# Two additions of exponentials per group, moved from GpSimd to VectorE in 30 groups

## The chip, the cores and the metric

The kernel runs on one core of a Trainium2 chip. The metric is the device time of one execution in microseconds (us). Engines: TensorE (PE, with its weight loads as PEld), VectorE (DVE), ScalarE (ACT), GpSimd (POOL), and SyncE (SP), which starts the DMAs.

## The reference

One transformer layer on 2048 tokens of width 512: the normalised tokens go through causal attention (16 heads of 32) and beside it through a feed-forward part with 4-bit weights; both are added to the input. The change lies in the attention:

```
scores = einsum('bhqd,bhkd->bhqk', q, k) * scale
scores = where(causal, scores, finfo.min)
probs = softmax(scores, axis=-1)          # exp(s - row max) / sum over keys
attn = einsum('bhqk,bhkd->bhqd', probs, v)
x = x + attn @ w_o.T + ffn(xn)
```

The sum over the keys in the softmax is what is divided by: one number for each query and head. The additions of this document make it.

## The kernel before, in words

Three stages follow one another: normalisation and the projections (up to about 140 us of the span), attention (to about 727 us), and the output projection with the feed-forward part.

**Attention** works on 8 pairs of heads. Within a pair, `STEPS` lists 40 steps: for each of four chunks of 512 queries (`qc`), the tiles of 128 keys (`kt`) up to the diagonal. Four steps make a **group** (`GS`), so there are 80 groups, 0 to 79, ten for each pair. Groups 0, 2, 5 and 9 of a pair are **diagonal**: they hold the four key tiles that the causal mask cuts, and their steps get narrower (512, 384, 256, 128 queries).

In each step, for each head of the pair: TensorE makes the transposed scores, keys by queries (`scores_t`, line 1041, on the diagonal with a mask, line 1050), in three PSUM banks; ScalarE takes exponentials into one of 16 buffers `e_sb` (`exps`, line 819), one group ahead of what follows; TensorE multiplies them with V (`product_v`, line 1067). Step j of group k+1 is scored and exponentiated while TensorE is in group k.

**The row maxima** that the exponentials need come from a second set of scores, queries by keys, made up to 48 products ahead: the units. TensorE writes a unit into one of four banks of `p_s` (`scores`, line 1013), VectorE takes its maximum over the keys (`unit_max`, line 902, or 898 with the mask), and only then is the bank free (`bank_free`). Eight units fall to a group, spread by `some_units` over the group's transposed scores, seven before the products by V and the last behind them. Group 72 has six and 73 to 79 have none. When the maxima of a chunk are complete, VectorE joins them (`row_max`, line 909), GpSimd splits them into three bf16 parts in five small operations (`split`, lines 751 to 759), and TensorE turns them (line 1023).

**The row sums.** Exponentials are first added elementwise over the steps of a group, and only the sum goes through TensorE (`row_sums`, line 1084, against ones). The list `ADDS[k]` has the additions of group k, each for one head (0 or 1) in turn. A group off the diagonal has four: numbers 0 and 1 add steps 0 and 1, numbers 2 and 3 add steps 2 and 3, and VectorE then **joins** the two halves for each head (`join_sums`, line 957). A diagonal group has six: 0 and 1 add the part of step 0 that step 1 covers and step 1, and 2 to 5 add steps 2 and 3 into the same sum, in place; there is no join. The sums lie in six slots (`SUM_BUFS`), and an addition that starts a sum waits till its slot has been read (`needs`). GpSimd does the additions (line 736) in groups with units. In groups without units VectorE does half of them (line 947).

**Order of the work.** Each engine's program is written out in a loop over the groups and runs in that order. GpSimd in turn k: additions from number 2 on of group k, additions 0 and 1 of group k+1, splits, and in some groups of pairs 2, 4, 6 and 7 a normalisation of an earlier pair's result (line 770). VectorE in turn k: the maxima of the group's units, the join before the last one, joined row maxima, its own additions. ScalarE overwrites a buffer only when the addition that read it is done (`used_up`). In the last groups VectorE also divides (`divide`, lines 929 and 934) and splits the output weights (line 985), and GpSimd splits the attention result (line 775).

## Time and profile before

| | us |
|---|---|
| median of three runs | 1799.53 (1797.9 to 1799.81) |
| the profiled execution | 1800.45, span 1798.7 |
| TensorE busy | 1763.6 (98%) |
| VectorE busy | 1237.7 (69%) |
| GpSimd busy | 752.2 (42%) |
| ScalarE busy | 715.2 (40%) |
| GpSimd's additions of exponentials, line 736 (the form from two buffers) | 304.4, 244 of them |

The table is over all three stages. In the 40 slices of the page, attention is about slices 5 to 16; there GpSimd's tenths are 8, VectorE's 8 and 9, TensorE's 9. Shares over the whole span hide that. In a timeline row the first number is the start, the second the length, both in us; `x2` is two instructions in one row, whose length is from the start of the first to the end of the last, and the bracket at the end is idle time of the engine before it and what ended it. In rows of waits the numbers are the total, the count and the longest.

### The profile page before, as it was taken

Reading aid. Unit: us, or ns where it says so; the run is one execution under the profiler, and the core shown is the slowest. Engines: PE = TensorE matmul, PEld = TensorE weight load, DVE = VectorE, ACT = ScalarE, POOL = GpSimd, SP = SyncE. Lnnn points to the kernel's source line nnn. Section 1 sums busy time; section 2 is a strip of 40 time slices with the busy share of each in tenths; the row PEclk is TensorE's granted clock in tenths of the full one; section 3 lists DMA queues with packets and bytes.
Section 4 is the critical chain, followed back from the end, with each engine's and each line's share of the span. In section 5 each row is a group of like instructions: output and inputs, shape, how many; then the busy total and the mean of one; then the engine's idle time right before and its main releaser. Section 6 shows DMA issues by size and latency. Waiting matters only on the chain.

```text
span 1798.7 us, 28378 instructions
## 1 busy us (share of the span) xinstructions
PE 1763.6 (98%) x10176; PEld 1346.1 (75%) x10176; DVE 1237.7 (69%) x1834; ACT 715.2 (40%) x1171; POOL 752.2 (42%) x716
## 2 busy tenths in 40 slices
PE   7999999999999999999999999999999999999998
PEld 6886666656556556888888888888888888888887
DVE  5526888888888889686676567567567666666654
ACT  3324666666666665233223232323233223222322
POOL 1432888888888886122122222222222222222221
PEclk9999999999999999999999999999999999999999
DMA  8775044144143111511110110110110010010002
GB/s 280 223 230 156 10 105 84 28 105 84 29 105 83 29 40 60 182 30 36 35 35 0 35 35 0 35 35 0 35 35 14 21 35 28 7 35 0 1 1 94
DMA packets 75615, 108.55 MB, mean 60 GB/s; under 512 B 24912, under 2 KB 44992, under 8 KB 72384
## 3 DMA queue, kind: packets, MB, share of 16 engines
q1 hardware_dynamic: 75520, 107.34, 22.1%
q8 instruction: 53, 0.87, 0.2%
q14 instruction: 42, 0.34, 0.1%
HBM read 74.04 MB, written 29.59 MB: 58 GB/s over the span
## 4 chain that ended last, share of the span: by engine, by line
PE 59%; DVE 0%; ACT 0%; issue 0%; ACTq 0%
PE p_up L52 7%; PE p_v L52 7%; PE p_up L51 7%; PE p_v L51 7%; PE p_up L50 7%; PE p_v L50 7%; PE p_s L51 6%; PE p_s L52 6%; PE p_s L50 6%; PE p_s L345 0%; PE p_s L339 0%; PE p_s L340 0%; PE p_v L339 0%; PE p_v L345 0%; PE p_v L340 0%; PE p_up L339 0%
## 5 line engine op out<-in xcount | busy, mean ns | idle before, releaser
L1392 POOL TENSOR_SCALAR poly<-poly 128x1024 f32<-128x1024 f32 (+1 forms) x65 | 72.4, 1114 | 800.8 <-ACT poly L1349 800.8
L736 POOL TENSOR_TENSOR e_sum<-e_sb 128x512 f32<-128x512 f32 (+1 forms) x244 | 304.4, 1271 | 75.5 <-ACT e_sb L819 39.1
L902 DVE TENSOR_REDUCE max_part<-p_s 128x1 f32<-128x512 f32 x384 | 247.1, 683 | 62.2 <-PE p_s L1013 61.3
L819 ACT ACTIVATE e_sb<-p_v 128x512 f32<-128x512 f32 (+3 forms) x427 | 216.1, 549 | 119.6 <-PE p_v L1041 59.1
L1455 DVE SCALAR_TENSOR_TENSOR inter<-inter,gate 128x1024 f32<-128x1024 f32 (+1 forms) x65 | 78.6, 1209 | 241.1 <-ACT inter L1355 240.3
L50 PE MATMUL p_v<-xn_hi,w_hi 128*128 128x512 f32 x512 | 199.2, 389 | 0.0
L51 PE MATMUL p_v<-xn_lo,w_hi 128*128 128x512 f32 x512 | 199.2, 389 | 0.0
L52 PE MATMUL p_v<-xn_hi,w_lo 128*128 128x512 f32 x512 | 199.2, 389 | 0.0
L50 PE MATMUL p_up<-xn_hi,w_hi 128*128 128x512 f32 x512 | 199.2, 389 | 0.0
L51 PE MATMUL p_up<-xn_lo,w_hi 128*128 128x512 f32 x512 | 199.2, 389 | 0.0
L52 PE MATMUL p_up<-xn_hi,w_lo 128*128 128x512 f32 x512 | 199.2, 389 | 0.0
L1348 ACT ACTIVATE gate<-p_v 128x1024 f32<-128x1024 f32 (+1 forms) x65 | 66.0, 1015 | 332.7 <-PE p_v L52 332.7
L50 PE MATMUL p_s<-stack_hi,w_hi 128*128 128x512 f32 x504 | 196.1, 389 | 0.0
L51 PE MATMUL p_s<-stack_lo,w_hi 128*128 128x512 f32 x504 | 196.1, 389 | 0.0
L52 PE MATMUL p_s<-stack_hi,w_lo 128*128 128x512 f32 x504 | 196.1, 389 | 0.0
L1395 POOL TENSOR_TENSOR poly<-poly,gate 128x1024 f32<-128x1024 f32 (+1 forms) x65 | 179.5, 2761 | 5.4
L1067 PE MATMUL p_o<-e_sb,v_stack 128*32 128x256 f32 (+1 forms) x2304 | 149.4, 374 | 0.0
L1355 ACT ACTIVATE inter<-poly 128x1024 f32<-128x1024 f32 (+1 forms) x65 | 68.1, 1047 | 202.3 <-POOL poly L1395 202.3
L1475 DVE TENSOR_TENSOR acc<-acc,p_s 128x2048 f32<-128x2048 f32 x63 | 143.7, 2280 | 3.3 <-PE p_s L52 3.3
L898 DVE CUSTOM_DVE_ANT_0 recip<-p_s,score_mask 128x128 bf16<-128x128 f32 (+3 forms) x256 | 115.8, 485 | 37.2 <-PE p_s L1013 36.4
L819 ACT ACTIVATE e_sb<-p_st 128x512 f32<-128x512 f32 (+2 forms) x213 | 117.3, 551 | 58.2 <-PE p_st L1041 30.3
L1360 ACT ACTIVATE stack_hi<-inter 128x1024 fp32r<-128x1024 f32 (+1 forms) x65 | 68.1, 1048 | 163.0 <-DVE inter L1461 163.0
(190 smaller groups left out, 3486.7 us busy)
## 6 DMA issues: line engine op xcount, KB each, us to landing
k_stack<-qk_scratch SPq DMA_DIRECT2D x42, 256.0 KB, 7.6
qk_scratch<-out_hi SPq DMA_DIRECT2D x32, 256.0 KB, 2.6
qk_scratch<-out_lo SPq DMA_DIRECT2D x32, 256.0 KB, 3.3
q_stack<-qk_scratch SPq DMA_DIRECT2D x24, 256.0 KB, 6.5
xn_lo_scratch<-xn_lo SPq DMA_DIRECT2D x4, 1024.0 KB, 5.2
v_stack<-in_gate_up_s SPq DMA_DIRECT2D x64, 64.0 KB, 2.3
xn_lo<-xn_lo_scratch SPq DMA_DIRECT2D x4, 1024.0 KB, 13.8
scales<-in_gate_up_s SPq DMA_DIRECT2D x64, 64.0 KB, 2.5
```

The costliest lines, as they stand in the source:

```text
L50: nc.tensor.matmul(out, w_hi, x_hi, start=first, stop=False)
L51: nc.tensor.matmul(out, w_hi, x_lo, start=False, stop=False)
L52: return nc.tensor.matmul(out, w_lo, x_hi, start=False, stop=last)
L736: nc.gpsimd.tensor_tensor(*operands(k, i), ALU.add).then_inc(pool_summed, 1)
L819: nc.scalar.activation(e_sb[:, x % E_BUFS, 0:w], bank_st(x)[:, 0:w], ACT.Exp, scale=SCALE).then_inc(exp_done, 1)
L898: nc.vector.tensor_tensor_reduce(out=masked_scores[:, m % 2, 0:w], in0=p_s[:, slot[n] % S_BUFS, 0:w], in1=score_mask[:, W - w:], scale=1.0 ...
L902: nc.vector.reduce_max(part, p_s[:, slot[n] % S_BUFS, 0:w], AX.X).then_inc(maxed, 1)
L1067: last = nc.tensor.matmul(p_o[(2 * a + h) * D:(2 * a + h + 1) * D, 0, first - h * HALF:], v_stack[p % PB][:, kt, a, :], e_sb[:, (g * PIECE ...
L1392: nc.gpsimd.tensor_scalar(part_of(poly, h, parts), part_of(poly, h, parts), GELU_A, 1.0, ALU.mult, ALU.add).then_inc(poly_done, 1)
L1395: nc.gpsimd.tensor_tensor(part_of(poly, h, parts), part_of(poly, h, parts), part_of(gate, h, parts), ALU.mult).then_inc(poly_done, 1)
L1455: nc.vector.scalar_tensor_tensor(part_of(inter, h, parts), part_of(inter, h, parts), 1.0, part_of(gate, h, parts), ALU.add, ALU.mult).then ...
L1475: nc.vector.tensor_tensor(here, here, p_out[:, :, :], ALU.add).then_inc(added, 1)
```

## The change

VectorE makes additions 0 and 1 of group k+1 in front of the last maximum of group k, where group k is diagonal and has units (`EARLY[k + 1]`). In such a group GpSimd makes all the others. Where a group is not `EARLY`, the share is as before: that is, VectorE's own additions in groups 74 to 79. In group 73, which is `EARLY` and has no units, VectorE makes 0 and 1 instead of 2 and 3. Additions in place wait for the engine that made the one before (`needs` now gives the semaphore with the count).

```
--- before.py
+++ after.py
@@ -429,6 +429,8 @@
 
 
 
+
+    EARLY = [k > 0 and DIAG[GS * (k - 1) % NS] and len(units_of(k - 1)) > 0 for k in range(NG)]
     ADDS, first_sum, sum_group, made, added_to = [], [], [], {}, []
     by_pool = by_vector = 0
     for k in range(NG):
@@ -440,7 +442,7 @@
         first_sum.append(len(sum_group))
         sum_group += [k] * (2 if diag else 4)
         for i, (m, a, _, _) in enumerate(ADDS[k]):
-            vector = not units_of(k) and (a == 1 if diag else m >= 2)
+            vector = i < 2 if EARLY[k] else not units_of(k) and (a == 1 if diag else m >= 2)
             by_vector += vector
             by_pool += not vector
             made[k, i] = (vector, by_vector if vector else by_pool)
@@ -568,13 +570,14 @@
             m, a, _, x = ADDS[k][i]
             n = first_sum[k] + m
             if x is None:
-                return None, made[k, i - 2][1]
+                vector, count = made[k, i - 2]
+                return None, (vector_summed if vector else pool_summed, count)
             if n < SUM_BUFS:
-                return None, 0
+                return None, None
             group = sum_group[n - SUM_BUFS]
             if not DIAG[GS * group % NS] and n - SUM_BUFS < first_sum[group] + 2:
-                return (joined, JOINED_TO[group]), 0
-            return (rows_done, group + 1), 0
+                return (joined, JOINED_TO[group]), None
+            return (rows_done, group + 1), None
 
         def operands(k, i):
             m, a, y, x = ADDS[k][i]
@@ -588,7 +591,7 @@
             return e_sum[:, n % SUM_BUFS, 0:W - q0], e_sb[:, ((GS * k + x) * PIECES + a) % E_BUFS, skip:skip + W - q0], new
 
         def pooled_to(k, i):
-            return max(count for j in range(i + 1) for vector, count in [made[k, j]] if not vector)
+            return max([added_to[k - 1][0]] + [count for j in range(i + 1) for vector, count in [made[k, j]] if not vector])
 
 
         def v_slot(v):
@@ -732,7 +735,7 @@
                         if free:
                             pool.wait_ge(*free)
                         if earlier:
-                            pool.wait_ge(pool_summed, earlier)
+                            pool.wait_ge(*earlier)
                         nc.gpsimd.tensor_tensor(*operands(k, i), ALU.add).then_inc(pool_summed, 1)
 
             def split(p, r, before):
@@ -934,8 +937,8 @@
                         nc.vector.tensor_tensor(attn_rows(p, a, qc)[:, h * HALF:(h + 1) * HALF], o[rows, 0, :],
                                                 recip[rows, 0:HALF], ALU.mult).then_inc(divided, 1)
 
-            def sum_steps(k):
-                for i in range(len(ADDS[k])):
+            def sum_steps(k, part):
+                for i in range(len(ADDS[k]))[part]:
                     vector, count = made[k, i]
                     if vector:
                         dve.wait_ge(exp_done, exps_for(k, i))
@@ -943,7 +946,7 @@
                         if free:
                             dve.wait_ge(*free)
                         if earlier:
-                            dve.wait_ge(vector_summed, earlier)
+                            dve.wait_ge(*earlier)
                         nc.vector.tensor_tensor(*operands(k, i), ALU.add).then_inc(vector_summed, 1)
 
             def join_sums(k):
@@ -970,11 +973,13 @@
                 for n in units:
                     if n == units[-1]:
                         join_sums(k)
+                        if k + 1 < NG and EARLY[k + 1]:
+                            sum_steps(k + 1, slice(0, 2))
                     unit_max(n)
                     for p_, r in BATCHES[k]:
                         if n + 1 == p_ * NU + UNITS_TO[r]:
                             join_parts(p_, r)
-                sum_steps(k)
+                sum_steps(k, slice(2 if EARLY[k] else 0, None))
                 if not units:
                     join_sums(k)
                 if p == PAIRS - 1 and s in (20, 24, 28):
```

VectorE's instructions where group 10 (diagonal) ends and group 11 begins, before. Line 902 and 898 are maxima, 957 is the join, `max_part` 128x1 the second half of 898:

```order
L902 TENSOR_REDUCE max_part<-p_s 128x1 [waits scored] x6
L898 ISA recip,max_part<-p_s,score_mask 128x384 [waits maxed,scored]
L898 ISA max_part 128x1
L898 ISA recip,max_part<-p_s,score_mask 128x384 [waits maxed,scored]
L898 ISA max_part 128x1
L902 TENSOR_REDUCE max_part<-p_s 128x1 [waits scored]
L957 TENSOR_TENSOR e_sum<-e_sum 128x512 [waits pool_summed]
L957 TENSOR_TENSOR e_sum<-e_sum 128x512
L902 TENSOR_REDUCE max_part<-p_s 128x1 [waits scored]
```

The same place in the changed kernel, where the lines are 905, 901 and 960, and 950 is an addition of exponentials:

```order
L905 TENSOR_REDUCE max_part<-p_s 128x1 [waits scored]
L950 TENSOR_TENSOR e_sum<-e_sb 128x512 [waits rows_done,exp_done] x2
L905 TENSOR_REDUCE max_part<-p_s 128x1 [waits scored] x5
L901 ISA recip,max_part<-p_s,score_mask 128x384 [waits maxed,scored]
L901 ISA max_part 128x1
L901 ISA recip,max_part<-p_s,score_mask 128x384 [waits maxed,scored]
L901 ISA max_part 128x1
L905 TENSOR_REDUCE max_part<-p_s 128x1 [waits scored]
L960 TENSOR_TENSOR e_sum<-e_sum 128x512 [waits vector_summed,pool_summed]
L960 TENSOR_TENSOR e_sum<-e_sum 128x512
L905 TENSOR_REDUCE max_part<-p_s 128x1 [waits scored]
```

Two additions of group 11 stand in front of the last maximum of group 10; the rest keeps its order.

GpSimd at the same place, before: the two rows of additions in place of group 10, all four additions of group 11, and additions 0 and 1 of group 12 (128x384):

```order
L736 TENSOR_TENSOR e_sum<-e_sum,e_sb 128x256 [waits pool_summed,exp_done] x2
L736 TENSOR_TENSOR e_sum<-e_sum,e_sb 128x128 [waits pool_summed,exp_done] x2
L736 TENSOR_TENSOR e_sum<-e_sb 128x512 [waits rows_done,exp_done] x4
L736 TENSOR_TENSOR e_sum<-e_sb 128x384 [waits rows_done,exp_done] x2
```

And now (line 739), where additions in place of group 10 wait for VectorE's sums:

```order
L739 TENSOR_TENSOR e_sum<-e_sum,e_sb 128x256 [waits vector_summed,exp_done] x2
L739 TENSOR_TENSOR e_sum<-e_sum,e_sb 128x128 [waits pool_summed,exp_done] x2
L739 TENSOR_TENSOR e_sum<-e_sb 128x512 [waits rows_done,exp_done] x2
L739 TENSOR_TENSOR e_sum<-e_sb 128x384 [waits rows_done,exp_done] x2
```

Additions 2 and 3 of group 11 are left in one row of two.

VectorE at the end of the maxima, in groups 72 to 74, before. Line 985 splits output weights:

```order
L898 ISA max_part 128x1
L898 ISA recip,max_part<-p_s,score_mask 128x512 [waits maxed,scored]
L898 ISA max_part 128x1
L909 TENSOR_REDUCE row_max<-max_part 128x2x4 [waits max_split,maxed]
L985 TENSOR_TENSOR stack_lo<-wo_sb,stack_hi 128x512 [waits wo_hi_made]
L947 TENSOR_TENSOR e_sum<-e_sb 128x512 [waits rows_done,exp_done] x2
L957 TENSOR_TENSOR e_sum<-e_sum 128x512 [waits vector_summed,pool_summed]
L957 TENSOR_TENSOR e_sum<-e_sum 128x512
L985 TENSOR_TENSOR stack_lo<-wo_sb,stack_hi 128x512 [waits wo_hi_made]
```

And now, with lines 990 for the weights and 912 for `row_max`:

```order
L901 ISA recip,max_part<-p_s,score_mask 128x512 [waits maxed,scored]
L901 ISA max_part 128x1
L950 TENSOR_TENSOR e_sum<-e_sb 128x512 [waits joined,exp_done] x2
L901 ISA recip,max_part<-p_s,score_mask 128x512 [waits maxed,scored]
L901 ISA max_part 128x1
L912 TENSOR_REDUCE row_max<-max_part 128x2x4 [waits max_split,maxed]
L990 TENSOR_TENSOR stack_lo<-wo_sb,stack_hi 128x512 [waits wo_hi_made]
L960 TENSOR_TENSOR e_sum<-e_sum 128x512 [waits vector_summed,pool_summed]
L960 TENSOR_TENSOR e_sum<-e_sum 128x512
L990 TENSOR_TENSOR stack_lo<-wo_sb,stack_hi 128x512 [waits wo_hi_made]
```

The additions of group 73 stand in front of the last masked maximum, and the join of group 73 follows directly on a weight split.

## Rows read from the trace of the kernel before

**Rows 1.** busy us (instructions) of each engine in one window; columns as headed

```profile
core 0: us, PE busy (x) PEld busy (x) DVE busy (x) ACT busy (x) POOL busy (x), PEclk, DMA share, GB/s
230.00:300.00 70.00, 68.58 (x638) 42.19 (x637) 59.88 (x137) 44.61 (x96) 55.84 (x71) 1.00 0.36 77
```

**Rows 2.** TensorE's waits, 178 to 716 us: total, times, longest us

```profile
PE p_s L1013 <- DVE max_part L898: 3.3, 7, 0.7
PE p_s L1013 <- DVE max_part L902: 1.5, 3, 0.5
```

**Rows 3.** timeline of VectorE at the ends of groups 9, 10, 12, 15

```profile
start us, us, engine line op out<-in xcount [idle before <-releaser]
241.15 0.69 DVE L902 TENSOR_REDUCE max_part<-p_s 128x1 f32<-128x512 f32 x1 [2.49 <-PE p_s L1013]
...
247.53 0.69 DVE L902 TENSOR_REDUCE max_part<-p_s 128x1 f32<-128x512 f32 x1 [1.67 <-PE p_s L1013]
...
260.74 0.29 DVE L898 CUSTOM_DVE_ANT_0 recip<-p_s,score_mask 128x128 bf16<-128x128 f32 x1 [1.26 <-PE p_s L1013]
...
261.61 0.42 DVE L898 CUSTOM_DVE_ANT_0 recip<-p_s,score_mask 128x256 bf16<-128x256 f32 x1 [0.57 <-PE p_s L1013]
...
280.54 0.69 DVE L902 TENSOR_REDUCE max_part<-p_s 128x1 f32<-128x512 f32 x1 [1.39 <-PE p_s L1013]
```

**Rows 4.** timeline of ScalarE (group 11's exponentials), then GpSimd

```profile
244.26 1.15 ACT L819 ACTIVATE e_sb<-p_v 128x512 f32<-128x512 f32 x2
245.22 0.68 ACT L819 ACTIVATE e_sb<-p_st 128x512 f32<-128x512 f32 x1
...
243.03 5.00 POOL L736 TENSOR_TENSOR e_sum<-e_sb 128x512 f32<-128x512 f32 x4 [0.87 <-ACT e_sb L819]
...
280.48 5.01 POOL L736 TENSOR_TENSOR e_sum<-e_sb 128x512 f32<-128x512 f32 x4
```

**Rows 5.** timeline of TensorE in groups 11, 12, then VectorE in 12

```profile
249.12 0.48 PE L1013 MATMUL p_s<-k_stack,q_stack 96*128 96x512 f32 x1
...
249.84 0.38 PE L1041 MATMUL p_st<-q_stack,k_stack 128*128 128x256 f32 x1
...
256.59 0.63 PE L1013 MATMUL p_s<-k_stack,q_stack 96*128 96x512 f32 x2
...
255.32 2.48 DVE L902 TENSOR_REDUCE max_part<-p_s 128x1 f32<-128x512 f32 x4
```

**Rows 6.** timeline, GpSimd and VectorE at group 17; then all joins, grouped

```profile
290.92 2.98 POOL L736 TENSOR_TENSOR e_sum<-e_sb 128x512 f32<-128x512 f32 x2 [1.60 <-PE p_o L1084]
...
291.24 3.20 DVE L957 TENSOR_TENSOR e_sum<-e_sum 128x512 f32<-128x512 f32 x2
...
L957 DVE TENSOR_TENSOR e_sum<-e_sum 128x512 f32<-128x512 f32 x96 | 106.3, 1146 | 1.0 <-POOL e_sum L736 0.2
```

**Rows 7.** timeline of GpSimd and VectorE in group 26

```profile
349.32 5.46 POOL L736 TENSOR_TENSOR e_sum<-e_sb 128x512 f32<-128x512 f32 x4
...
351.89 3.45 DVE L957 TENSOR_TENSOR e_sum<-e_sum 128x512 f32<-128x512 f32 x2
```

**Rows 8.** timeline of TensorE: groups 27 and 28, and 18

```profile
355.99 0.51 PE L1013 MATMUL p_s<-k_stack,q_stack 96*128 96x512 f32 x1 [0.50 <-DVE max_part L902]
...
363.13 0.50 PE L1013 MATMUL p_s<-k_stack,q_stack 96*128 96x512 f32 x1 [0.67 <-DVE max_part L898]
...
294.98 0.50 PE L1013 MATMUL p_s<-k_stack,stack_lo 96*128 96x512 f32 x1 [0.30 <-DVE max_part L898]
```

**Rows 9.** timeline of VectorE, GpSimd, TensorE at attention's end

```profile
667.57 1.30 DVE L947 TENSOR_TENSOR e_sum<-e_sb 128x512 f32<-128x512 f32 x2
...
670.80 3.43 DVE L947 TENSOR_TENSOR e_sum<-e_sb 128x512 f32<-128x512 f32 x2
...
678.45 0.56 DVE L947 TENSOR_TENSOR e_sum<-e_sb 128x384 f32<-128x384 f32 x1 [1.33 <-PE p_o L1084]
...
667.12 0.61 POOL L751 CAST max_cols<-row_max 128x8 bf16<-128x8 f32 x1 [2.89 <-DVE row_max L909]
...
670.28 3.40 POOL L736 TENSOR_TENSOR e_sum<-e_sb 128x512 f32<-128x512 f32 x2
...
711.37 1.08 PE L1084 MATMUL p_o<-e_sum,ones 128*32 128x256 f32 x8 [3.00 <-DVE e_sum L957]
```

More of the change, by code:

```diff
@@ L425, in attention @@
     slot = {what: n for n, what in enumerate(ring)}
+    EARLY = [k > 0 and DIAG[GS * (k - 1) % NS] and len(units_of(k - 1)) > 0 for k in range(NG)]
     ADDS, first_sum, sum_group, made, added_to = [], [], [], {}, []
@@ L442, in attention @@
         for i, (m, a, _, _) in enumerate(ADDS[k]):
-            vector = not units_of(k) and (a == 1 if diag else m >= 2)
+            vector = i < 2 if EARLY[k] else not units_of(k) and (a == 1 if diag else m >= 2)
             by_vector += vector
@@ L570, in needs @@
             if x is None:
-                return None, made[k, i - 2][1]
+                vector, count = made[k, i - 2]
+                return None, (vector_summed if vector else pool_summed, count)
             if n < SUM_BUFS:
-                return None, 0
+                return None, None
             group = sum_group[n - SUM_BUFS]
             if not DIAG[GS * group % NS] and n - SUM_BUFS < first_sum[group] + 2:
-                return (joined, JOINED_TO[group]), 0
-            return (rows_done, group + 1), 0
+                return (joined, JOINED_TO[group]), None
+            return (rows_done, group + 1), None
         def operands(k, i):
@@ L590, in pooled_to @@
         def pooled_to(k, i):
-            return max(count for j in range(i + 1) for vector, count in [made[k, j]] if not vector)
+            return max([added_to[k - 1][0]] + [count for j in range(i + 1) for vector, count in [made[k, j]] if not vector])
         def v_slot(v):
@@ L734, in sum_steps @@
                         if earlier:
-                            pool.wait_ge(pool_summed, earlier)
+                            pool.wait_ge(*earlier)
                         nc.gpsimd.tensor_tensor(*operands(k, i), ALU.add).then_inc(pool_summed, 1)
@@ L935, in divide, with sum_steps @@
                                                 recip[rows, 0:HALF], ALU.mult).then_inc(divided, 1)
-            def sum_steps(k):
-                for i in range(len(ADDS[k])):
+            def sum_steps(k, part):
+                for i in range(len(ADDS[k]))[part]:
                     vector, count = made[k, i]
@@ L945, in sum_steps @@
                         if earlier:
-                            dve.wait_ge(vector_summed, earlier)
+                            dve.wait_ge(*earlier)
                         nc.vector.tensor_tensor(*operands(k, i), ALU.add).then_inc(vector_summed, 1)
@@ L972, in _ @@
                         join_sums(k)
+                        if k + 1 < NG and EARLY[k + 1]:
+                            sum_steps(k + 1, slice(0, 2))
                     unit_max(n)
@@ L976, in _ @@
                             join_parts(p_, r)
-                sum_steps(k)
+                sum_steps(k, slice(2 if EARLY[k] else 0, None))
                 if not units:
```

## The prediction

> **What bounds the kernel now.** I read the views from coarse to fine. A 70 us window in the middle of the attention stage [rows 1] shows TensorE busy for 68.58 us at full granted clock, VectorE for 59.88, GpSimd for 55.84: TensorE bounds the stage, VectorE has some 10 us in 70 left, GpSimd 14. Next, TensorE's waits between 178 and 716 us: its scores wait 4.8 us in all for VectorE's maxima (3.3 and 1.5, [rows 2]), and once, at 711.37, it waits 3.00 us for a join of VectorE's [rows 9]. TensorE is almost never held up by GpSimd, so relief of GpSimd brings nothing by itself. It can only help through VectorE, and VectorE is the engine that gets the work. So the question is where VectorE has room, and how much lateness TensorE forgives.
>
> **What is removed, added and moved.** Groups are numbered 0 to 79, ten for each pair of heads. In the 30 groups whose forerunner is diagonal and has maxima (1, 3, 6, then 10, 11, 13, 16, 20, 21, ...) additions 0 and 1 pass to VectorE. In group 73 VectorE in turn gives up additions 2 and 3. By the lists of additions that the program makes, GpSimd goes from 368 to 310 and VectorE from 16 to 74. VectorE does the two right before the last maximum of the diagonal group. There it idles today until TensorE, busy with the products by V, sends the last score: 2.49 us in group 9, 1.67 in group 10, 1.26 in group 12, 1.39 in group 15, and the same in every later pair [rows 3].
>
> **Price of two additions.** Where GpSimd is not adding, two of 128x512 take VectorE 1.30 us (at 667.57, [rows 9]). Where VectorE is not, four take GpSimd 5.00 us, so two 2.5 (at 243.03, [rows 4]). When both add at once they take turns: GpSimd started at 290.92 and took 2.98 for two, VectorE started 0.32 us later and took 3.20 for two [rows 6]. So the pair on VectorE costs 1.30 us or 3.20 us, depending on whether GpSimd is adding at that moment. A mean over all joins would be neither.
>
> The Trainium skill (SBUF — State Buffer, "Who interferes with whom") says that a VectorE instruction with two inputs in SBUF and a GpSimd instruction that reads SBUF block one another whole, and that whoever is first decides. By a reading in which both merely slow down, the pair would cost 2 x 1.146 = 2.3 us (the mean join in the window's list, [rows 6]), VectorE would be 0.6 us late after group 10, and nothing would be lost there. By the skill's rule it is the 3.2 us above. The rows at 290.92 and 291.24 agree with the rule, with 3.20 us.
>
> **Groups 9, 12 and 15: no cost.** In 9 there is 2.49 us of room. In 12 the additions start as VectorE gets free, 1.26 us before the score, and overrun by 0.04 us, and the next idle time is 0.57 us [rows 3]. In 15 they fit, 1.30 into 1.39. GpSimd does not collide here: after its own diagonal additions it has the splitting of the maxima, which waits for VectorE's row_max and lasts till 280.48 (small operations), and only then additions [rows 4]. If that cover is gone, each costs like group 10.
>
> **Group 10: the loss.** GpSimd has no splitting here. Freed of additions 0 and 1 of group 11 (today it does all four in one run, from 243.03 to 248.03), it starts addition 2 when its exponentials are there: ScalarE finishes them at 245.4 and 245.9 [rows 4]. VectorE gets free at 245.86 (247.53 less 1.67 of idle time, [rows 3]), 0.4 us after GpSimd has begun: the situation of 290.92 again. So 3.20 us from 245.8, to 249.0; the last maximum starts at 249.0 and not at 247.53, about 1.4 us late.
> TensorE writes scores into four banks, so the fourth score of group 11 (249.12) needs the bank of that maximum (ended 248.22): room 0.90 us. I allow 0.05 from the end of a maximum to the score behind it and take 0.05 off the lateness for rounding: 1.35 + 0.05 - 0.90, about 0.5 us of wait. ScalarE's wait at 249.84 (0.12 us, [rows 5]) is swallowed by it, so 0.36 is left. VectorE's remaining lateness against TensorE is then about 0.6 us (1.4 less what TensorE waited, less the short idle times between maxima), and I let 0.15 of it go in the rest of group 11: 0.45. In group 12 the sixth score (256.83, the second of the pair of matmuls at 256.59) stands 0.21 behind the end of its maximum (256.62, the second of four from 255.32, [rows 5]): 0.45 + 0.05 - 0.21 = 0.29 us more. Sum 0.65 us in each of eight places (groups 0, 10, ..., 70): **+5.2 us**. Bounds: 0, if the two run unhindered (1.30 < 1.67); and 1.4 us each, 11.2 us, if none of the lateness is forgiven.
>
> **Odd pairs: the gain.** In group 26 (also 46 and 66) GpSimd is behind today because it also normalises: additions of 26 and 27 from 349.32 to 354.8, across VectorE's join of 26, which takes 3.45 us where two operations alone would take 1.3 [rows 7]. TensorE pays 0.50 us at 355.99, and at 363.13 it pays 0.67 where the even pair pays 0.30 (294.98) [rows 8]. Without additions 0 and 1 of group 26 (2.5 us) the rest starts some 2 us earlier, and the additions of 27 end near 352.5. The join still meets the end of one, and then the normalisation, but ends some 0.5 us earlier. Value 0.50 + 0.37 = 0.87 us, three times: **-2.6 us**. Bounds: 0 (the normalisation, itself an addition-like operation, merely takes the place of the additions) and all of the 4.8 us that scores wait for maxima [rows 2].
>
> **The end of attention.** There are no maxima from group 73 on, and VectorE does half of the additions, both joins and the divisions. From 678.45 on it shows no idle time until its last join, for which TensorE waits 3.00 us [rows 9]. Whatever reaches 678.45 late comes out at the end, less 1.33 us of idle time there. Additions 0 and 1 of group 73 move in front of the last maximum of group 72, where VectorE idles like in the other diagonal groups, and cost nothing. But additions 2 and 3 now lie with GpSimd, behind the splitting (from 667.12; about 1.8 us once VectorE's two additions no longer lie across it) and take 2.5: until 671.4. The join of 73 starts then, not right behind VectorE's own additions at 668.9, and in turns with GpSimd's additions of 74, so 3.4 us (the price that additions 2 and 3 of group 74 pay today, [rows 9]) to 674.8. Behind it on VectorE are a split of the output weights (with the normalisation ahead of it on GpSimd, to 676.7), two additions (1.3), the join of 74 (1.3) and another weight split (0.6): 679.8. So the work of 678.45 starts 1.35 us late, and the 3.00 us become about 4.4: **+1.4 us**. TensorE itself needs the join of 73 only in front of the products of group 74, whose row sums release VectorE at 678.45, so that has room. Bounds: -3.0 (the wait disappears) and +3.4 (the whole shift).
>
> Nothing else moves the end: the row sums of the diagonal groups find their additions earlier than today, and DMAs are not touched.
>
> **Sum.** +5.2 - 2.6 + 1.4 = +4.0 us. The profiled execution took 1800.45 us (span 1798.7); with +4.0 it would take 1804.5. The median of the runs is 0.9 lower, 1799.53: **1803.5 us**, 0.22% slower. About 0.2% (3.6 us) is what a measurement of this kernel can tell from no change.
>
> **The rivals.**
> 1. The additions on VectorE are free, since they fall into its idle time: group 10 costs nothing. For it: the 58 additions at 0.65 are 38 us, and rows 3 show idle time at each place. Against it: 0.4 us head start of GpSimd. Time: 1799.5 - 2.6 + 1.4 = 1798.3, no change to be measured.
> 2. Relief of GpSimd wins: the joins no longer meet its additions in odd pairs, and the end of attention is reached without the last wait, because VectorE has two additions fewer there. -2.6 - 3.0 = -5.6: 1793.9, faster. It decides if GpSimd finishes additions 2 and 3 of group 73 before about 669.5. Against it: they stand behind the splitting, which ends near 669 at the earliest.
> 3. The lateness is not forgiven: each place costs 1.4 us, and the end takes the full 3.4: 1799.5 + 11.2 + 3.4 - 2.6 = 1811.5. It would take VectorE to be late in groups 11 and 12 with no idle time to recover; against it, the idle times of 1.26 and 0.57 us in group 12.
> 4. The change does not do what it says, as the exponentials of the next group come too late and VectorE waits in front of its last maximum: the exponentials it needs are finished 1 us before [rows 4]; I give it nothing of its own.
>
> **Chances.** Forecast 0.52 (its own range 1801 to 1806.5), rival 1 0.27, rival 2 0.09, rival 3 0.12. The range 1797.5 to 1809 takes in rival 1 and half of rival 3. Slower by over 0.2% (above 1803.1): half of the forecast's case and more, and rival 3: 0.47. Faster (below 1795.9): 0.10. Within: 0.43.
>
> **What the changed profile would show.** Right: VectorE's two additions in group 10 take near 3.2 us, with GpSimd's first addition of group 11 started before them, while those in groups 12 and 15 take 1.3; TensorE's waits on maxima have new entries of about 0.5 us near 249 and every 67 us on, and 0.3 near 257; the 0.50 at 355.99 is gone or halved; the 3.00 on the last join is above 4. Wrong: the additions in group 10 take 1.3 us (then rival 1), the last wait is shorter than 3.0 (rival 2), or waits of over 0.5 us stand in groups 13 to 16 too (rival 3).

## The result and the profile after

The changed kernel takes 1804.7 us (median of seven runs, 1803.9 to 1806.05), against 1799.53 before: ratio 1.0031, 95% interval 1.0019 to 1.0042. It is 5.2 us slower. Its profiled execution spans 1802.9 us, 4.2 more than the one before.

The same 70 us window as in [rows 1] of the changed kernel (columns: busy us and instructions of PE, PEld, DVE, ACT, POOL, then granted clock, DMA share, GB/s):

```profile
230.00:300.00 70.00, 68.04 (x629) 42.27 (x632) 65.85 (x146) 44.62 (x96) 47.68 (x62) 1.00 0.35 76
```

VectorE went from 59.88 to 65.85 us of 70, GpSimd from 55.84 to 47.68. TensorE, which bounds the stage, lost 0.54 us of work in the window. (VectorE's busy time includes what an addition waits for its turn inside its row, so the 6 us more are not all work.)

TensorE's waits for maxima, 178 to 700 us, in the changed kernel (total, times, longest), where [rows 2] had 3.3 and 1.5 us:

```profile
PE p_s L1018 <- DVE max_part L905: 3.0, 10, 0.3
PE p_s L1028 <- DVE max_part L905: 2.7, 14, 0.2
PE p_s L1018 <- DVE max_part L901: 2.3, 7, 0.3
```

The second row is the matmul that turns the row maxima (line 1028, before 1023). [rows 2] leave it out; before, in the same stretch, it was

```profile
PE p_s L1023 <- DVE max_part L902: 1.3, 7, 0.2
```

All waits for maxima together went from 6.1 to 8.0 us.

The place of the forecast loss, VectorE in groups 10 and 11 (timeline: start, length, us):

```profile
246.02 3.23 DVE L950 TENSOR_TENSOR e_sum<-e_sb 128x512 f32<-128x512 f32 x2
249.17 3.07 DVE L905 TENSOR_REDUCE max_part<-p_s 128x1 f32<-128x512 f32 x5
```

GpSimd there:

```profile
245.73 2.96 POOL L739 TENSOR_TENSOR e_sum<-e_sb 128x512 f32<-128x512 f32 x2 [3.78 <-ACT e_sb L822]
```

and TensorE:

```profile
247.23 0.50 PE L1018 MATMUL p_s<-k_stack,q_stack 96*128 96x512 f32 x1
...
249.90 0.50 PE L1018 MATMUL p_s<-k_stack,q_stack 96*128 96x512 f32 x1 [0.34 <-DVE max_part L905]
...
252.39 0.38 PE L1028 MATMUL p_s<-ident_bf,max_cols 128*64 128x128 bf16 x4 [0.20 <-DVE max_part L905]
...
254.56 0.50 PE L1018 MATMUL p_s<-k_stack,q_stack 96*128 96x512 f32 x1
```

GpSimd begins 0.29 us before VectorE, the two then take turns, and VectorE's pair takes 3.23 us. It runs straight into the last maximum of group 10, where there had been 1.67 us of idle time. TensorE waits 0.34 us for the bank, and 0.20 more at the matmul that turns the row maxima. To see what a group costs I compare when TensorE sends its last score. Those of groups 10 and 11 were sent at 246.99 and 253.85 before and at 247.23 and 254.56 now: 0.24 and 0.71 us later, a step of about 0.46 us in group 11. It returns within 0.01 us in groups 21, 31, 41, 51, 61 and 71. I call such a difference from one group to the next a **step**. The steps of the attention stage with maxima are: +0.46 seven times, +0.76 three times (groups 25, 45, 65), -0.62 to -0.66 three times (27 and 28, 47 and 48, 67 and 68, together), +0.08 once. Sum +3.6 us. Steps also leave out what differs before attention: the last score of group 0 lies between 1.07 us earlier and 2.35 us later than before in the profiled executions of this document.

The step of +0.76 was not forecast. VectorE and GpSimd in groups 22 to 24 of the changed kernel:

```profile
327.55 1.30 DVE L950 TENSOR_TENSOR e_sum<-e_sb 128x512 f32<-128x512 f32 x2
...
340.61 2.90 DVE L960 TENSOR_TENSOR e_sum<-e_sum 128x512 f32<-128x512 f32 x2 [0.82 <-POOL e_sum L739]
```

```profile
327.47 0.22 POOL L754 CAST max_cols<-row_max 128x8 bf16<-128x8 f32 x1 [5.36 <-DVE row_max L912]
327.77 0.53 POOL L756 TENSOR_TENSOR rest<-row_max,max_cols 128x8 f32<-128x8 f32 x1
328.37 0.56 POOL L758 CAST max_cols<-rest 128x8 bf16<-128x8 f32 x1
...
338.06 4.90 POOL L739 TENSOR_TENSOR e_sum<-e_sb 128x512 f32<-128x512 f32 x4
```

GpSimd now idles 5.36 us in front of the splitting of the maxima, which waits for VectorE's `row_max`. The additions taken from it would have filled that time; its work behind does not start earlier. On the contrary: VectorE's pair at 327.55 lies across the splitting, whose second and third operation take 0.53 and 0.56 us in place of 0.20 and 0.22. GpSimd reaches the additions of group 24 later, and VectorE's join of 24 waits 0.82 us and then meets GpSimd's next additions: 2.90 us, where it took 2.10 without a wait before. TensorE, 1.23 us behind the kernel before at that time, is 1.98 us behind at the same matmul of group 25 (344.08 before, 346.06 now).

The end of attention. VectorE's join of group 73, GpSimd before it, and TensorE's last waits:

```profile
675.27 3.43 DVE L960 TENSOR_TENSOR e_sum<-e_sum 128x512 f32<-128x512 f32 x2 [3.71 <-POOL e_sum L739]
```

```profile
671.03 0.61 POOL L754 CAST max_cols<-row_max 128x8 bf16<-128x8 f32 x1 [7.68 <-DVE row_max L912]
...
672.71 5.44 POOL L739 TENSOR_TENSOR e_sum<-e_sb 128x512 f32<-128x512 f32 x4
```

```profile
716.04 0.64 PE L1089 MATMUL p_o<-e_sum,ones 128*32 128x256 f32 x8 [3.75 <-DVE e_sum L960]
...
718.61 0.30 PE L1089 MATMUL p_o<-e_sb,ones 128*32 128x128 f32 x2 [0.42 <-DVE e_sum L950]
```

The join waits 3.71 us for GpSimd, whose additions 2 and 3 of group 73 stand behind the splitting, and takes 3.43. Against [rows 9] TensorE's wait went from 3.00 to 3.75, with 0.42 behind it (`only3` below, whose end of attention is as before, has 0.49 there too). These two executions can't be compared directly, though, as the granted clock shows (columns as above, before and then after, 668 to 676 us, and 708 to 716 or 712 to 720):

```profile
668.00:676.00 8.00, 6.92 (x44) 3.02 (x44) 7.79 (x9) 5.00 (x11) 6.92 (x7) 0.79 0.20 77
708.00:716.00 8.00, 5.00 (x55) 2.64 (x48) 7.69 (x10) 0.00 (x0) 5.01 (x4) 0.79 0.46 134
```

```profile
668.00:676.00 8.00, 7.31 (x74) 3.68 (x65) 3.71 (x9) 5.51 (x11) 4.68 (x8) 1.00 0.59 183
678.00:686.00 8.00, 7.56 (x61) 4.62 (x61) 7.90 (x7) 5.07 (x12) 6.50 (x6) 0.79 0.01 2
712.00:720.00 8.00, 3.84 (x55) 2.12 (x48) 7.69 (x10) 0.00 (x0) 4.96 (x4) 1.00 0.51 147
```

The execution before had two stretches at 1.2 GHz at the end of attention, the one after had one, so part of the loss is hidden in the pair of profiles: 4.2 us there, 5.2 between the medians.

### The profile page after: what moved, and what is told of

Read it like the earlier page. It is cut to its first block, busy times and chain, and to the rows that moved or that the text cites. A ratio compares the mean times of both kernels' runs of the same rounds, so it can differ in the third digit from the quotient of the medians.

```text
span 1802.9 us, 28450 instructions
## 1 busy us (share of the span) xinstructions
PE 1764.1 (98%) x10176; PEld 1345.8 (75%) x10176; DVE 1284.4 (71%) x1892; ACT 716.1 (40%) x1171; POOL 693.6 (38%) x658
## 4 chain that ended last, share of the span: by engine, by line
PE 59%; DVE 0%; ACT 0%; issue 0%; ACTq 0%
PE p_v L50 6%; PE p_up L50 6%; PE p_up L52 6%; PE p_v L51 6%; PE p_v L52 6%; PE p_up L51 6%; PE p_s L50 6%; PE p_s L52 6%; PE p_s L51 6%; PE p_s L340 0%; PE p_s L339 0%; PE p_s L345 0%; PE p_v L339 0%; PE p_v L340 0%; PE p_v L345 0%; PE p_up L339 0%
## 5 line engine op out<-in xcount | busy, mean ns | idle before, releaser
L739 POOL TENSOR_TENSOR e_sum<-e_sb 128x512 f32<-128x512 f32 (+1 forms) x186 | 237.3, 1301 | 81.7 <-ACT e_sb L822 50.5
L1447 DVE SCALAR_TENSOR_TENSOR w_lo<-weight,w_hi 128x1024 fp32r<-128x1024 f32 x48 | 92.4, 1926 | 56.9 <-ACT w_hi L1346 56.9
```

Source lines behind the costliest of these rows:

```text
L739: nc.gpsimd.tensor_tensor(*operands(k, i), ALU.add).then_inc(pool_summed, 1)
L1447: nc.vector.scalar_tensor_tensor(w_lo[par][:, m, :, :], weight[:, :, :], CODE_SCALE, w_hi[par][:, m, :, :].bitcast(F32), ALU.mult, ALU.sub ...
```

## The experiments

Each is an edit of the changed kernel, compared with the kernel before run on the same chip. Times are compared by their medians, which is good to about 2 us from one kernel to another; steps are good to 0.05 us where the clock is the same. The medians mix executions with more and with fewer stretches at 1.2 GHz. Of the kernel before, measured beside the first four experiments, 19 executions with a mean granted clock of 0.999 have a median of 1797.91 us, and four with 0.997 have 1801.17. That is as much as most effects here, so the argument rests on steps and rows first. The first ones choose the groups with the early pair by a condition in one line:

```
-    EARLY = [k > 0 and DIAG[GS * (k - 1) % NS] and len(units_of(k - 1)) > 0 for k in range(NG)]
+    EARLY = [k > 0 and DIAG[GS * (k - 1) % NS] and len(units_of(k - 1)) > 0 and CONDITION for k in range(NG)]
```

**The second groups alone** (`only1`, CONDITION `k % 10 == 1`).

> VectorE makes additions 0 and 1 early only in the second group of each pair (1, 11, 21, ..., 71). Theory (the two engines' additions exclude one another, and GpSimd's head start of 0.4 us makes VectorE's pair cost 3.3 us in place of 1.3): TensorE falls behind by 0.46 us in each of groups 11, 21, ..., 71 and nowhere else, so +3.2 us against the kernel before, about 1802.8. Rival (the cost is spread over all 58 moved additions, 5.2 us / 58 each): 16 of them make +1.4 us, 1801.0, with steps of TensorE elsewhere too. Rival (free in idle time): 1799.5.

Measured: 1801.87 against 1799.0, ratio 1.0020 (1.0010 to 1.0029). The steps are 0.46 us in groups 11, 21, ..., 71, and nowhere else is there one above 0.06. The +2.9 us (interval 1.8 to 5.2) fit 7 x 0.46 = 3.2; a cost spread over all additions gave 1.4 and steps elsewhere too.

**All but the second groups** (`no1`, CONDITION `k % 10 != 1`).

> The change without the second groups of the pairs. Theory: the seven steps of 0.46 us go, 1804.7 - 3.2 = 1801.5; the step of 0.76 us in groups 25, 45 and 65 stays. Rival (spread over all additions): 1804.7 - 1.4 = 1803.3.

Measured: 1802.45, ratio 1.0019 (1.0008 to 1.0031). The seven steps are gone and +0.73, +0.70, +0.73 in groups 25, 45, 65 remain. The time fell by 2.2 us, between the two expectations; the steps decide for the theory.

**The same work without overlap** (`held1`).

```
                         if earlier:
                             pool.wait_ge(*earlier)
+                        if EARLY[k] and k % 10 == 1 and i == 2:
+                            pool.wait_ge(vector_summed, made[k, 1][1])
```

> The changed kernel, and in groups 1, 11, ..., 71 GpSimd's addition 2 waits until VectorE has made its two. The same work with no overlap. Theory: VectorE's pair takes 1.3 us, fits in 1.67 us, TensorE's step of 0.46 us in 11, 21, ... vanishes: 1804.7 - 3.2 = 1801.5, unless GpSimd, 1.8 us later, now meets the join of group 11. Rival (VectorE is late for another reason than GpSimd's additions: exponentials, slots, or its own load): the step stays, 1804.7.

Measured: 1801.97, ratio 1.0019 (1.0010 to 1.0029); 2.7 us less than the changed kernel. VectorE and GpSimd in group 10:

```profile
246.03 1.28 DVE L952 TENSOR_TENSOR e_sum<-e_sb 128x512 f32<-128x512 f32 x2
247.79 0.69 DVE L907 TENSOR_REDUCE max_part<-p_s 128x1 f32<-128x512 f32 x1 [0.48 <-PE p_s L1020]
```

```profile
247.48 4.61 POOL L741 TENSOR_TENSOR e_sum<-e_sb 128x512 f32<-128x512 f32 x4 [5.52 <-PE p_o L1091]
```

The pair takes 1.28 us in place of 3.23, 0.48 us of idle time are left in front of the maximum, and there is no step in 11, 21, ..., 71. VectorE does as many additions as in the changed kernel, and GpSimd starts its own 1.75 us later. So it is the overlap, not VectorE's load, that cost 0.46 us. Nor were the exponentials late (rival 4): the pair starts without idle time, at 246.02 and at 246.03.

**The seventh groups alone** (`only6`, CONDITION `k % 10 == 6`).

> VectorE makes additions 0 and 1 early only in the seventh group of each pair (6, 16, 26, ..., 66). Theory: no step against TensorE; the joins of 26, 46 and 66 get less in the way of GpSimd, and TensorE gains 0.6 us (as in the changed kernel) to 0.87 us (as forecast) three times: 1799.5 - 1.9 to 2.6, about 1797.3. Rival (relief of GpSimd brings nothing, what was gained in groups 27 and 28 of the changed kernel is only the 0.76 us lost before, partly given back): 1799.5.

Measured: 1796.02 against 1799.0, ratio 0.9984 (0.9975 to 0.9994): faster. Steps -0.52 and -0.35 us in groups 27 and 28, -0.50 and -0.36, -0.54 and -0.34 in the later ones: -0.87 each time, which is the forecast term. VectorE's join of group 26, then TensorE's first wait behind it:

```profile
350.79 2.94 DVE L960 TENSOR_TENSOR e_sum<-e_sum 128x512 f32<-128x512 f32 x2
```

```profile
361.16 0.50 PE L1018 MATMUL p_s<-k_stack,q_stack 96*128 96x512 f32 x1 [0.33 <-DVE max_part L901]
```

The join takes 2.94 us where it took 3.45 [rows 7]; of TensorE's waits in [rows 8] the 0.50 is gone and the 0.67 is 0.33. The rival falls.

**The fourth groups alone** (`only3`, CONDITION `k % 10 == 3 and k < 73`).

> VectorE makes additions 0 and 1 early only in the fourth groups (3, 13, 23, ..., 63). Theory (in these groups GpSimd idles before the splitting anyway, so it gains nothing; VectorE's pair lies across the splitting and lengthens it by 0.7 us; in pairs 2, 4 and 6, where GpSimd also normalises, this reaches the join of 24, 44, 64): TensorE falls behind by 0.75 us in groups 25, 45, 65, and the 0.50 and 0.67 us of groups 27 and 28 do not get smaller: 1799.0 + 2.2 = 1801.2. Rival (the step comes from all of GpSimd's altered order together, the late groups 21 and 22 above all): no step in 25, 1799.0.

Measured: 1799.13 against 1799.41, ratio 0.9999 (0.9990 to 1.0009). The steps of +0.77, +0.71, +0.75 in groups 25, 45, 65 are there, so the fourth groups make them. But groups 27, 47 and 67 give back 0.60, 0.53 and 0.58, which I had not expected. TensorE, held up in 25, no longer waits in 27; I read it as one wait in place of the other, which no run isolates. (A step of +1.67 in group 28 is a stretch at 1.2 GHz at 365 us.)

**All but the fourth groups** (`no3`, CONDITION `k % 10 != 3 or k == 73`).

> The change without the fourth groups (3, 13, ..., 63). Theory (the step of 0.75 us in 25, 45, 65 comes from them and eats the gain of groups 26, 46, 66): that step goes, and the waits in 27 and 28 fall by 0.87 us as in the kernel that changes the seventh groups alone: TensorE's balance in each of these pairs changes from +0.14 to -0.87, 1804.7 - 3.0 = 1801.7. Rival (the parts add up: the fourth groups alone changed nothing that can be measured): 1804.7.

Measured: 1802.29 against 1799.88, ratio 1.0019 (1.0008 to 1.0029). No step in 25, and -0.86, -0.85, -0.85 in groups 27 and 28, 47 and 48, 67 and 68. Two small ones appear in 58 and 69 (+0.3 each). 2.4 us less than the changed kernel, where 3.0 were expected: the gain of the seventh groups had been eaten by the fourth, though the fourth alone change nothing that can be measured. What makes the two small steps is open.

**Group 73 alone** (`only73`, CONDITION `k == 73`).

> Only group 73 is changed: VectorE makes 0 and 1 in front of the last maximum of group 72, GpSimd makes 2 and 3. Theory (the join of 73 waits 3.7 us for GpSimd, and the lateness reaches the last join less the idle time at 678): TensorE's 3.0 us wait for the join of group 78 becomes 3.8 to 4.4, 1799.0 + 0.8 to 1.4 = about 1800.1. Rival (VectorE has two additions fewer behind the maxima): the wait falls below 3.0, under 1799.0.

Measured: 1803.51 against 1799.41, ratio 1.0019 (1.0008 to 1.0030), between 1.4 and 5.4 us by the interval; more than expected. Part of that is the clock: six of the ten executions have a granted clock of 0.996 or 0.997 (1802.97 to 1807.09 us), and the four with 0.998 or more have a median of 1800.81, 1.5 us above the 20 such executions of the kernel before (1799.28). TensorE's wait for the last join is 6.15 us in the profile, but that is the slowest of the ten, with stretches at 1.2 GHz at 503, 673 and 714 us.

**All but group 73** (`no73`, CONDITION `k != 73`).

> The change without group 73. Theory (the late join of 73 costs 2.1 to 2.7 us at the end of attention where TensorE's clock is not halved): 1804.7 - 2.4 = 1802.3; TensorE's only large wait there is 3.0 to 3.3 us for the last join. Rival (the end costs 1.4 us, as forecast): 1803.3. Rival (nothing; the long times of the kernel that changes 73 alone came from the halved clock): 1804.7.

Measured: 1801.83 against 1799.88, ratio 1.0011 (1.0002 to 1.0021), 2.9 us less than the changed kernel. The last wait is 3.24 us. For the size at full clock, the time from TensorE's last score (a unit of group 72) to its first matmul of the next stage serves: 61.95 us in the kernel before (665.59 to 727.54), with two stretches at 1.2 GHz; 60.13 in `only3`, whose program is the same there and whose clock is 1.00 in all of it; 62.84 in `no1`, with group 73 changed and the clock also 1.00. That is +2.7 us. More executions agree: with no stretch at 1.2 GHz before TensorE waits for the last join, its first matmul behind the last join starts 44.33 to 44.35 us after the last score in `only3`, `only6` and `no73`, and 47.03 and 47.04 us after it in `no1` and `no3`. TensorE's waits in `no1`:

```profile
688.00 0.30 PE L1089 MATMUL p_o<-e_sb,ones 128*32 128x128 f32 x2 [1.38 <-DVE e_sum L950]
693.57 0.50 PE L1046 MATMUL p_v<-q_stack,k_stack 128*128 128x512 f32 x1 [0.59 <-ACT e_sb L822]
714.03 0.64 PE L1089 MATMUL p_o<-e_sum,ones 128*32 128x256 f32 x8 [3.25 <-DVE e_sum L960]
```

The lateness comes out already at the row sums of group 75 (1.38 us) and the exponentials behind it (0.59), and not only at the last join. `no3` has the same two (1.39 and 0.60). The changed kernel and `held1` have neither; both had a stretch at 1.2 GHz ahead of that place (at 680 and 677 us), in which TensorE itself was slow.

VectorE's side of it. In `no1`, the join of 74 and the first addition of group 75, and then that addition in `only3`:

```profile
679.99 3.29 DVE L960 TENSOR_TENSOR e_sum<-e_sum 128x512 f32<-128x512 f32 x2
...
684.35 0.81 DVE L950 TENSOR_TENSOR e_sum<-e_sb 128x384 f32<-128x384 f32 x1
```

```profile
678.28 1.36 DVE L950 TENSOR_TENSOR e_sum<-e_sb 128x384 f32<-128x384 f32 x1
```

Counted from the last score (667.00 and 666.83), the addition of group 75 starts 17.35 us later in `no1` and 11.45 in `only3`: VectorE is 5.9 us late, because the join of 73 came late and because it met GpSimd's work again behind it. By the last join it has won back 3.2 us, for instance in four products of the divisions that take 2.79 us where they take 4.49 in `only3`, and 2.7 us are left. And in `only3` there is no idle time in front of that addition. The 1.33 us before it in [rows 9] stood in an execution whose TensorE had just had a stretch at 1.2 GHz (670 to 673 us). `only1` and `hold89`, with a stretch at the same place, have 1.31 and 1.36 us of idle time there; `only6`, without one, has none.

**One addition instead of two for VectorE at the end** (`six_tail`, CONDITION `k % 10 == 6`).

```
-            vector = i < 2 if EARLY[k] else not units_of(k) and (a == 1 if diag else m >= 2)
+            vector = i < 2 if EARLY[k] else not units_of(k) and (a == 1 if diag else m == 3)
```

> The early pair only in groups 6, 16, ..., 66, and in the groups off the diagonal that have no units (73, 74, 76, 77, 78) VectorE makes one addition (number 3) and GpSimd three, in place of two and two. Theory (VectorE has no idle time from 678 us to its last join, GpSimd has 1 to 3 us in each group): VectorE saves 5 additions of 0.65 to 1.7 us, so TensorE's 3.0 us wait for the last join goes nearly away: 1796.0 - 2.5 = 1793.5. Rival (additions take turns, so the join now waits for GpSimd as in group 73 of the change): no gain or a loss, 1796.0 or more.

Measured: 1799.36, ratio 1.0002 (0.9993 to 1.0012): 3.3 us slower than the seventh groups alone. My theory fell, and the rival that I had named stands. VectorE's join of group 73, in `six_tail` and then in `only6`, whose last scores lie 0.03 us apart:

```profile
666.80 3.44 DVE L960 TENSOR_TENSOR e_sum<-e_sum 128x512 f32<-128x512 f32 x2 [2.16 <-POOL e_sum L739]
```

```profile
665.32 1.31 DVE L960 TENSOR_TENSOR e_sum<-e_sum 128x512 f32<-128x512 f32 x2
```

GpSimd now makes three additions of group 73 behind the splitting. The join waits 2.16 us for them and then takes turns with the ones that follow. The products of the first division start at 683.02 instead of 679.20. TensorE feels it here:

```profile
688.54 0.51 PE L1046 MATMUL p_v<-q_stack,k_stack 128*128 128x512 f32 x1 [2.09 <-ACT e_sb L822]
```

and ScalarE, on which it waits:

```profile
687.40 0.60 ACT L834 ACTIVATE o_sb<-p_o 128x512 f32<-128x512 f32 x1 [3.24 <-DVE acc L937]
```

ScalarE holds its exponentials behind a copy that waits for VectorE's divisions. The last wait is 3.79 us.

**GpSimd held back where VectorE joins** (`six_hold8`, and `six_hold89` with `(8, 9)`; both with the early pair in the seventh groups alone). If overlap is the cost, it should help at the joins that overlap already in the kernel before [rows 6, 8]:

```
                         if earlier:
                             pool.wait_ge(*earlier)
+                        if i == 0 and k < 70 and k % 10 in (8,):
+                            pool.wait_ge(joined, JOINED_TO[k - 1])
```

> The early pair only in groups 6, 16, ..., 66, and GpSimd's additions 0 and 1 of groups 8, 18, ..., 68 wait until VectorE has joined groups 7, 17, ..., 67. No addition changes its engine. Theory (turns at the join: 3.2 us for two additions that alone take 1.3): the join of group 17 takes 1.3 us, VectorE enters group 18 1.9 us earlier, and TensorE's 0.3 us wait there goes, some of the 0.3 us at the turned maxima of 18 and 19 too: 0.3 to 0.6 us in each of seven pairs, 1796.0 - 2 to 4 = about 1793. Rival (GpSimd, 1.5 us later, hands its lateness to the join of 18): no gain or a loss, 1796 or more.

> As the kernel before it, and GpSimd's additions 0 and 1 of groups 9, 19, ... also wait for the join of 8, 18, .... Theory: the join of 18 falls from 2.4 to 1.3 us too, and all 0.6 us of waits in groups 18 and 19 go: 1796.0 - 4 = 1792. Rival (GpSimd's chain additions, splitting, additions in place becomes late for the row sums of 19 and 20, some 2 us of room): waits of TensorE on GpSimd appear, and it is slower than with the hold in group 8 alone.

Measured: 1801.13, ratio 1.0011 (1.0001 to 1.0021) for the first, and 1791.79 against 1799.88, ratio 0.9959 (0.9944 to 0.9973), for the second. The joins of 17 and 18 in the second:

```profile
291.41 1.29 DVE L962 TENSOR_TENSOR e_sum<-e_sum 128x512 f32<-128x512 f32 x2
...
298.36 1.28 DVE L962 TENSOR_TENSOR e_sum<-e_sum 128x512 f32<-128x512 f32 x2
```

GpSimd there:

```profile
292.87 5.01 POOL L741 TENSOR_TENSOR e_sum<-e_sb 128x512 f32<-128x512 f32 x4 [3.22 <-DVE e_sum L962]
299.81 1.98 POOL L741 TENSOR_TENSOR e_sum<-e_sb 128x384 f32<-128x384 f32 x2 [1.93 <-DVE e_sum L962]
```

With 291.24 of [rows 6] at 3.20, the join takes 1.29 now. Both kernels gain 0.64 us in group 8 and in 18. The first loses it in pairs 2, 4 and 6, where GpSimd also normalises: +1.7, +3.0 and +3.2 us in groups 29, 49, 69. Its profile also has stretches at 1.2 GHz near 505 us (group 49) and near 642 us (group 69), so the full 3.0 and 3.2 are not the hold's alone. All ten executions of `six_hold8` have a granted clock of 0.995 to 0.997, where 16 of the 24 of the kernel before have 0.999. At 0.997 on both sides it is the faster one: 1799.74 (three) against 1801.72 (six). So its 1801.13 is the price of those stretches as much as that of the hold; why this version had more of them is open. Its join of group 28:

```profile
365.48 2.89 DVE L962 TENSOR_TENSOR e_sum<-e_sum 128x512 f32<-128x512 f32 x2 [1.52 <-POOL e_sum L741]
```

It waits 1.52 us for the delayed GpSimd and then still takes turns with it. With the second hold the wait is the same but the join behind it is free, and the step is +0.41 us. In `six_hold89` VectorE also waits 1.00 us in group 22 for the DMA that brings the sums back (a step of +0.97). It is the fastest version, 12.9 us below the changed kernel and 8.1 below the one before.

**The holds alone** (`hold89`, CONDITION `False`).

> No addition changes its engine against the kernel before; only the two holds of GpSimd (additions 0 and 1 of groups 8, 9, 18, 19, ... wait for VectorE's join of the group before). Theory (the gain of the last kernel is the sum of order and of the early pair in groups 6, 16, ...): the 0.80 us in groups 18 and 19 of the pairs 0, 1, 3 and 5 stay, the 0.55 us in groups 27, 47 and 67 goes: 1791.8 + 2 to 3 = 1794.3. Rival (without the early pair GpSimd's lateness in the normalising pairs 2, 4 and 6 grows through the holds, so that they cost there): 1797 or more. Rival (the hold alone carries all): 1791.8.

Measured: 1795.59 against 1800.68, ratio 0.9968 (0.9956 to 0.9979). No addition has changed its engine, and the kernel is 0.32% faster than before. It lies between the theory (1794.3) and the first rival (1797 or more). The steps are -0.66 and -0.16 us in groups 8 and 9 and their like, and -1.01, +0.41 in 28, 29, 48, 49, 68, 69; the 0.5 us that TensorE waits in groups 27 and 47 stay, as the theory says. One step of +1.4 us in group 22 is of another kind: VectorE waits 1.42 us there for the DMA that brings the sums back.

## Why the prediction was right, point by point

The forecast was 1803.5 us, the measured time is 1804.7. The direction and the main mechanism were right; that the number fits so closely is luck, as the terms show.

**The price of two additions** was right: 3.20 forecast, 3.23 measured in group 10, 1.28 with GpSimd held. In groups 12 and 15 they took 1.30 and 1.28, as forecast. Reading both engines as merely slower would have given 2.3. The Trainium skill (SBUF — State Buffer, "Who interferes with whom") says that a VectorE instruction with two inputs in SBUF and a GpSimd instruction that reads SBUF exclude one another. The trace agrees: the pair takes 3.23 with overlap and 1.28 without, and the edit between the two is one wait. From GpSimd's start to VectorE's end the four additions took 3.52 us (245.73 to 249.25), a little less than the 3.8 that 1.3 and 2.5 add up to.

**Group 10's loss**, forecast 0.65 us in eight places (5.2), is 0.46 in seven (3.2). The 0.5 us wait at the fourth score was 0.34, followed by 0.20 at the turned maximum, which I had not listed. The second part, 0.29 us in group 12, was wrong. The join of group 11, before and after:

```profile
252.36 1.84 DVE L957 TENSOR_TENSOR e_sum<-e_sum 128x512 f32<-128x512 f32 x2
```

```profile
253.72 1.56 DVE L960 TENSOR_TENSOR e_sum<-e_sum 128x512 f32<-128x512 f32 x2
```

It takes 0.28 us less, and TensorE falls no further behind in group 12. Group 1 shows no step either. So the place and the mechanism hold and the term was 2 us too large.

**Groups 9, 12, 15 at no cost**: right at the place, wrong one step on. The sentence that failed is that GpSimd "does not collide here: after its own diagonal additions it has the splitting of the maxima". The splitting was taken as cover; it is itself slowed by VectorE's pair, and in pairs 2, 4 and 6 nothing behind it has room. +0.76 us, three times.

**The gain of -2.6 us in odd pairs** is there when nothing else is changed (`only6`: 3 x 0.87 = 2.6 by the steps, 3.0 us by the medians). In the changed kernel it is -0.62 three times, beside the +0.76: net +0.4 where I had -2.6.

**The end**, forecast +1.4, is +2.7 at full clock. The medians give 2.9 with and without group 73 in the changed kernel, and 1.5 for group 73 alone at an equal clock. The chain to the join was right: it started 4.2 us after the splitting began (671.03 to 675.27; forecast 4.3) and took 3.43. Two things failed behind it. The first is "Whatever reaches 678.45 late comes out at the end, less 1.33 us": the 1.33 us belonged to a stretch at 1.2 GHz in the one profile that I read, and at full clock they are not there. The second is the way from the join of 73 to the additions of 75. It was put at 5.0 us, with two additions and the join of 74 at 1.3 each, and took 8.2 in `no1`, where the join of 74 alone met GpSimd and took 3.29. The 5.9 us of lateness did not all come out: 3.2 were won back on the way to the last join, which the prediction had ruled out. That 2.7 is near the 1.35 + 1.33 of the forecast is therefore no proof of its chain.

The sum was near because two of its errors stand against each other, which is luck: 2 us too much in group 10, and 3 + 1.3 us too little in the odd pairs and at the end. From the steps it is 3.2 + 0.4 (with the +0.1 of group 22) + 2.7 = 6.3 us, and 5.2 was measured, with an interval of 3.4 to 7.6.

Of the rivals, the first (free in idle time) is excluded by `only1` and `held1`, the second (relief of GpSimd wins) is what `only6` does and the whole change doesn't, the third (1811.5 us, 12.0 above the kernel before) is excluded by the result. The fourth (exponentials too late) gave no idle time in front of the pair.

## What to carry to other kernels

Idle time of an engine is room for work only if the engines that share something with it are quiet at that moment. Before moving an operation into a gap, look at what its partner does in those microseconds after the move, not before it. Where two engines exclude one another, order them by a wait, so that the one whose result is awaited goes first: here the wait alone brought 0.3%, more than any move of work. But see where the lateness of the engine that is held comes out: with one hold instead of two, the next join met it, at +1.7 us in group 29. And relief of an engine counts only behind its next wait for somebody else. Last, idle time read from a single profile may belong to that execution: check it in a second one, at a place where the granted clock is the same.

## What was not expected of the hardware

Stretches at the lower of the two clock levels come and go between executions of nearly the same program. At the end of attention the granted clock was 0.79 on average from 668 to 676 us before, when TensorE had been busy 7.78 of the 8 us from 660 to 668, and 1.00 there in the changed kernel. In `only3` one began at 365 us, where TensorE had been busy 7.10 us of the 8 from 357 to 365. One such stretch cost 1.7 us: from TensorE's last score to the start of its wait for the last join it is 42.78 us before and 41.10 in `only3` with the clock at 1.00. What sets them off was not tried and stays open.

Their place goes with the length of the wait for the last join:

| a stretch at 1.2 GHz between the last score and TensorE's wait for the last join | end of attention as before | group 73 changed |
|---|---|---|
| none | 3.24, 3.23, 3.24 (`only3`, `only6`, `no73`) | 3.25, 3.23 (`no1`, `no3`) |
| 4.3 to 4.4 us after the last score | 3.00, 2.99, 3.00 (before, `only1`, `hold89`) | 6.15 (`only73`) |
| 10.0 to 10.7 us after it | 1.75, 0.60 (`six_hold8`, `six_hold89`) | 3.75, 3.83 (changed kernel, `held1`) |

So the 0.60 us in `six_hold89` need not come from its holds, which end in group 69, and a last wait can't be compared between executions with different rows of this table. How a stretch at one place makes the wait longer and at another shorter is not settled.
